# Float32r split of the row maxima moved from GpSimd to VectorE in an attention and expert kernel

## The reference

```python
xn = _layernorm(x)
q = xn @ Wq + bq;  latent = xn @ Wl + bl
k = latent @ Wk + bk;  v = latent @ Wv + bv          # 16 heads of 8
attn = softmax(q k^T * SCALE);  a = (attn v) @ Wo + bo
# experts: top 2 of 16, gate = min(gate, 7), up = clip(up, -7, 7)
out_e = ((up + 1) * gate * sigmoid(gate * 1.702)) @ Wd + bd
x = x + a + sum_e cw[e] * out_e
```

## Time and profile before

| | |
|---|---|
| three executions | 516.75, 517.58, 518.36 us |
| the profiled execution | 515.9 us, span of its instructions 514.0 us |
| TensorE busy | 453.2 us (88%), 2681 matmuls |
| VectorE busy | 374.6 us (73%) |
| ScalarE busy | 309.4 us (60%) |
| GpSimd busy | 192.9 us (38%) |
| mean granted TensorE clock | 0.913 |

### The profile page before, as it was taken

How to read it: one execution, slowest core, us unless ns; L and a number is a source line. 1 busy time by engine, 2 the same in 40 slices (tenths; PEclk the granted TensorE clock), 3 DMA queues, 4 the chain that set the end, 5 groups by cost and what they waited for, 6 DMA issues and landing times.

```text
span 514.0 us, 8995 instructions
## 1 busy us (share of the span) xinstructions
PE 453.2 (88%) x2681; PEld 209.3 (41%) x2681; DVE 374.6 (73%) x725; ACT 309.4 (60%) x356; POOL 192.9 (38%) x240
## 2 busy tenths in 40 slices
PE   0998984998989899989898989898989889799885
PEld 0554441333434344444444444444444434353243
DVE  8479992768888888888888878888888776764011
ACT  1541022477777686768686868686868644448840
POOL 6035876004141414141414141414141461824870
PEclk9976557789999999999999999999999988979966
DMA  8465512500544655304502443041004020101200
GB/s 239 126 120 179 101 44 87 162 3 1 129 123 121 189 102 111 104 1 78 109 22 83 86 100 104 3 82 22 21 3 91 16 59 7 39 22 43 57 23 25
DMA packets 39298, 39.01 MB, mean 76 GB/s; under 512 B 4998, under 2 KB 34792, under 8 KB 38376
## 3 DMA queue, kind: packets, MB, share of 16 engines
q1 hardware_dynamic: 35808, 33.74, 26.3%
q0 software_dynamic: 2432, 4.72, 3.9%
q10 hardware_dynamic: 1032, 0.23, 0.3%
HBM read 23.73 MB, written 13.89 MB: 73 GB/s over the span
## 4 chain that ended last, share of the span: by engine, by line
PE 59%; POOL 11%; DVE 11%; ACT 8%; issue 6%; another core or an unknown queue 2%; DMA 1%; ACTq 0%; SPq 0%; DVEq 0%; POOLq 0%
PE banks L987 17%; PE banks L970 16%; PE banks L1035 11%; DVE half_max L810 7%; ACT probs L674 5%; PE banks L1056 3%; PE banks L1054 3%; POOL th L545 2%; POOL up L546 2%; POOL up L528 2%; PE banks L1019 1%; PE banks L1017 1%; POOL th L544 1%; POOL up L541 1%
## 5 line engine op out<-in xcount | busy, mean ns | idle before, releaser
L810 DVE TENSOR_REDUCE half_max<-banks 128x1 f32<-128x512 f32 x512 | 322.0, 685 | 52.9 <-PE banks L970 39.9
L674 ACT ACTIVATE probs<-banks 128x1024 f32<-128x1024 f32 x256 | 254.9, 1026 | 162.5 <-PE banks L1035 113.1
L970 PE MATMUL banks<-k_rows,q_rows 62*128 62x512 f32 x512 | 182.9, 484 | 14.6 <-DVE half_max L810 10.4
L1035 PE MATMUL banks<-q_rows,k_rows 64*128 64x512 f32 x512 | 141.7, 460 | 7.0 <-ACT probs L674 5.5
L987 PE MATMUL banks<-probs,v_pad 128*32 128x512 f32 x1024 | 142.4, 630 | 0.0
L970 PEld LDWEIGHTS banks<-k_rows,q_rows 62*128 62x128 f32 x512 | 87.9, 199 | 103.5 <-DVE half_max L810 72.0
L1035 PEld LDWEIGHTS banks<-q_rows,k_rows 64*128 64x128 f32 x512 | 63.1, 192 | 77.6 <-ACT probs L674 66.9
L528 POOL TENSOR_TENSOR gate<-gate,w_blk 128x512 f32<-128x512 f32 x12 | 12.6, 1048 | 108.3 <-ACT gate L658 108.3
L528 POOL TENSOR_TENSOR up<-up,w_blk 128x512 f32<-128x512 f32 x12 | 12.6, 1049 | 97.8 <-ACT up L660 97.8
L510 POOL DMA_INDIRECT x_table<-xn,place_u x32 | 31.1, 972 | 20.9 <-DVE place_u L792 11.5
L987 PEld LDWEIGHTS banks<-probs,v_pad 128*32 128x32 f32 x1024 | 20.7, 110 | 44.3 <-issue 35.3
(11 more groups left out here) (117 smaller groups left out, 345.2 us busy)
## 6 DMA issues: line engine op xcount, KB each, us to landing
w_blk<-in_wexp SPq DMA_DIRECT2D x48, 193.0 KB, 3.1
q_rows<-q_parts SPq DMA_DIRECT2D x28, 128.0 KB
k_rows<-k_parts SPq DMA_DIRECT2D x56, 64.0 KB
x_table<-zeros SPq DMA_DIRECT2D x1, 3072.0 KB, 12.5
x_rows<-x_table SPq DMA_DIRECT2D x12, 256.0 KB, 3.7
moe_table<-x_rows SPq DMA_DIRECT2D x12, 256.0 KB, 6.8
q_parts<-q SPq DMA_DIRECT2D x8, 256.0 KB
k_parts<-k SPq DMA_DIRECT2D x8, 256.0 KB
```

The costliest lines, as they stand in the source:

```text
L674: nc.scalar.activation(probs[:, (2 * s + part) % 4, :, :], banks[:, bank:bank + 2, :], ACT.Exp, scale=SCALE).then_inc(slot_free, 1)
L810: nc.vector.tensor_reduce(half_max[:, unit, row, half:half + 1], banks[:, ring_bank(job), :], AX_X, ALU.max).then_inc(ring_free, 1)
L970: pe.matmul(bank, q_rows[slot][rows, pair, q0:q0 + P], k_rows[slot][rows, pair, 512 * keys:512 * keys + 512], start=True, stop=True).then_ ...
L1035: mm = pe.matmul(banks[:, bank + u, :], k_rows[(unit // 2) % 2][rows, pair, P * kb:P * kb + P], q_rows[(unit // 2) % 2][rows, pair, 512 * ...
```

## The change

The two GpSimd instructions of `split_max` and its two calls go. VectorE makes the first part itself, by a second reduction of the same 32 columns that writes float32r directly into `max2`, and then subtracts. Between the two it waits on its own semaphore `s_negmax`, which now counts two for each unit. The semaphore `s_vz` is no longer used, and `max_job` gets the turn `t` as a further argument. TensorE's, ScalarE's and SyncE's lists are the same.

```diff
             def split_max(parity, done):
-                pool.wait_ge(s_negmax, done)
-                whole = neg_max[:, parity, :].rearrange("p (u r) -> p u r", u=2)
-                nc.gpsimd.tensor_tensor(max2[:, parity, :, 0, :], whole, zeros[:, 0:16].rearrange("p (u r) -> p u r", u=2),
-                                        ALU.add).then_inc(s_vz, 1)
-                pool.wait_ge(s_vz, done)
-                nc.gpsimd.tensor_tensor(max2[:, parity, :, 1, :], whole, max2[:, parity, :, 0, :].bitcast(F32),
-                                        ALU.subtract).then_inc(s_max2, 1)
-                pool.wait_ge(s_max2, done)
...
             for n in range(2 * TILES):
-                    split_max(0, 1)
...
             def pair(t, p, last):
-                if has_max_turn(p, last):
-                    unit = (2 * p + LEAD - 2) // KB
-                    split_max(unit % 2, 4 * t + unit + 1)
...
-            def max_job(base, job, ahead, m):
+            def max_job(base, job, ahead, m, t):
...
                     nc.vector.tensor_reduce(neg_max[:, unit, :], half_max[:, unit, :, :], AX_X, ALU.max,
                                             negate=True).then_inc(s_negmax, 1)
+                    nc.vector.tensor_reduce(max2[:, unit, :, 0, :], half_max[:, unit, :, :].rearrange("p (u r) k -> p u r k", u=2),
+                                            AX_X, ALU.max, negate=True).then_inc(s_negmax, 1)
+                    dve.wait_ge(s_negmax, 8 * t + 2 * (ahead // KB) + 2)
+                    nc.vector.tensor_tensor(max2[:, unit, :, 1, :], neg_max[:, unit, :].rearrange("p (u r) -> p u r", u=2),
+                                            max2[:, unit, :, 0, :].bitcast(F32), ALU.subtract).then_inc(s_max2, 1)
```

More of the change, by code:

```diff
@@ L282, in moe_attention_kernel @@
         s_first_k = sem("s_first_k")
-        s_vz = sem("s_vz")
         s_vpad = sem("s_vpad")
@@ L484, in fill_v @@
                     v_all[:, bass.ds(g, 1), :, :].rearrange("p o k (j d) -> p (o k) j d", d=DH)).then_inc(s_vpad, 1)
-            def split_max(parity, done):
-                pool.wait_ge(s_negmax, done)
-                whole = neg_max[:, parity, :].rearrange("p (u r) -> p u r", u=2)
-                nc.gpsimd.tensor_tensor(max2[:, parity, :, 0, :], whole, zeros[:, 0:16].rearrange("p (u r) -> p u r", u=2),
-                                        ALU.add).then_inc(s_vz, 1)
-                pool.wait_ge(s_vz, done)
-                nc.gpsimd.tensor_tensor(max2[:, parity, :, 1, :], whole, max2[:, parity, :, 0, :].bitcast(F32),
-                                        ALU.subtract).then_inc(s_max2, 1)
-                pool.wait_ge(s_max2, done)
             pool.wait_ge(s_krow[0], 2)
@@ L852, in _ @@
                     maxima_turned(BEFORE_JOBS, TURN_OF_FIRST - BEFORE_JOBS, 0)
-                max_job(BEFORE_JOBS, job - BEFORE_JOBS, ahead, m)
+                max_job(BEFORE_JOBS, job - BEFORE_JOBS, ahead, m, 0)
             def pair(base, job, t, p, last):
@@ L857, in pair @@
                 for n, (ahead, m) in enumerate(maxima[:5]):
-                    max_job(base, job + n, ahead, m)
+                    max_job(base, job + n, ahead, m, t)
                 job += len(maxima[:5])
```

## The result

The changed kernel takes 521.51 us, the median of 20 executions (516.52 to 525.35). The kernel before took 517.62 us beside it (median of 20, 514.11 to 522.36). The ratio is 1.0066, with a 95% interval of 1.004 to 1.0093: slower by 0.7%, and outside the range of the forecast. The profiled execution has a span of 520.1 us and took 521.86 us; that of before had 514.0 and 515.9.

The account below looks back on a forecast made before the run. TensorE was taken as the bound (59% of the chain of waits), partly waiting for GpSimd's late split. Loop 9.0 - 1.6, plus 0.6 at the head, gave 8.0 us: 517.58 - 8.0 = 509.6 us, range 505.8 to 514.5.

Parts of the forecast that it names:

- The step that failed: Last turn: the last chain goes over TensorE, not the gathers, so gathers starting at once change 0, within 1.5 us.
- Rival 3: Head or last turn: the head's stop stays, or gathers running together hold up VectorE or ScalarE; 1 to 3 us lost; 12%.
- The loop: Three loop turns: nine TensorE waits for GpSimd's split shrink, gaining 9.0 us, less 1.6 us for delay on VectorE.
- The held subtraction: VectorE's two-input subtraction beside GpSimd's instructions in the loop: a possible wait for GpSimd, counted as nothing in the sum.
- Rival 1: Loop: the subtraction waits until GpSimd's running L544 ends, 0.37 or 0.52 us late, 3.8 us in all; 511.8 us; 34%.
- The register delay: VectorE in the loop: waiting on a register-held value delays the run of five 0.2 us, eight times, 1.6 us.
- the bare sum of 0.42: VectorE in the loop: reduction, wait and subtraction let the next max job start 0.42 us behind L814 at the shortest.
- The 9.0: Loop: the gain in us from nine TensorE waits at the transpose of the maxima, before VectorE's delays.
- Rival 2: Loop: the subtraction also waits for GpSimd's next instruction, L545; run of five 1.74 us late, 524.9 us; 6%.
- The head: First unit: without the split among GpSimd's scatters, these and VectorE's long stop come earlier; 0.6 us gained, between 0 and 0.9.
- The range's ends: Whole kernel: 505.8 us with full 9.0, 0.9 at the head, 1.5 in the last turn; 514.5 with rivals 1 and 3.

Follow-up runs that it names:

- Giving back the brake: The changed kernel, with GpSimd again waiting for VectorE's reduced maxima at the two old places in the last turn: 506.04 us, ratio 0.9844.
- the last turn alone: The kernel before, with only the last turn's two splits moved from GpSimd to VectorE: 524.78 us, ratio 1.0224.
- the one-input version: The changed kernel, with a third reduction of the 32 columns in place of the subtraction: 516.92 us, ratio 1.006.
- the spread version of the kernel before: The kernel before, split still on GpSimd, with gathers spread over the last turn's pairs and a pause in the head's scatters: 506.18 us, ratio 0.9843.
- the unaltered kernel: The changed kernel itself, run again in a set where the kernel before took 492.84 us: 487.01 us, ratio 0.9862.

## Why the prediction was wrong, step by step

**The step that failed** is the one on the last turn: "the last chain goes over TensorE to `y` at 510.61 us [...] not over the gathers, so I put this at 0, within 1.5 either way". It measured +12.7 us, the sum of +12.2, +10.4 and -9.9 in its three stretches. The argument looked only at whether somebody waits for the gathers' data. It missed that the gathers, while they are issued, stop the engines that set the time, and that TensorE's clock falls beside the stops. Moreover showed two waits of 11.12 and 13.42 us that would vanish with 16 gathers queued behind them, and the earlier trace rows had shown beside the scatters, which are such DMAs too, a stop of 9.66 us. With its price read from there, one such stop in the last turn would have forecast some 9 us more, 518 to 519. That is near to what came, but partly by luck: several stops and the slower clock lost more, and the end of the last turn gave 9.9 us back. Giving back the brake (0.9844) against the last turn alone (1.0224) shows this cause from both sides.

**Rival 3** had the mechanism in words, "gathers that now run together hold up VectorE or ScalarE", but was priced at 1 to 3 us and given 12%. Its argument against itself, "that the gathers stood beside the same work before", did not hold: they had stood beside it parted.

**The loop** went by the sum. It forecast 9.0 - 1.6 = 7.4 us; the milestones give 6.7. Where a wait had been, two transposes are 24.6 us apart instead of 25.4 (324.73 to 349.34 after, 330.35 to 355.74 before), close to the forecast 0.8. The first pass of the loop varies by some us between profiles of one and the same list (the second transpose to the 14th takes 301.4 to 309.3 us in the kernels with the change), so one pair of profiles proves little here. The later passes don't vary: from the 8th transpose to the 12th, a whole turn with three of the nine places, takes 101.7 to 101.8 us in all three kernels that keep the split on GpSimd in the loop and 99.4 to 99.6 in the 15 that have the change with its subtraction. That is 2.3 us a turn, 6.9 in three.

**The held subtraction.** The rule of the Trainium skill, SBUF — State Buffer, on engine ports was right here (0.40 to 0.58 us beside L532 against 0.17), and I had put the sum on the other side. Rival 1's sign came true: L805 ends with GpSimd's instruction. Two turns, GpSimd's row first:

```profile
122.45 0.62 POOL L532 TENSOR_SCALAR th<-th 128x512 f32<-128x512 f32 x1
147.11 0.62 POOL L532 TENSOR_SCALAR th<-th 128x512 f32<-128x512 f32 x1
...
146.90 0.19 DVE L800 TENSOR_REDUCE neg_max<-half_max 128x16 f32<-128x32 f32 x1
147.21 0.54 DVE L805 TENSOR_TENSOR max<-neg_max,max 128x16 fp32r<-128x16 f32 x1
147.67 3.07 DVE L796 TENSOR_REDUCE half_max<-banks 128x1 f32<-128x512 f32 x5
```

L532 ends at 123.07 and L805 at 122.70 + 0.40 = 123.10; in the second turn the ends are 147.73 and 147.75. The wait is inside the instruction's length and not in a bracket before it. The run of five starts 0.64 and 0.77 us behind L800, where I forecast 0.4 to 0.8. But the loss of 0.37 to 0.52 us at each place that rival 1 took from it is too high: the one-input version takes 98.95 us from the 8th transpose to the 12th, 0.57 less than the changed kernel's 99.52, or 0.2 at each of the three places.

**The register delay** of 0.2 us, guessed, is not there: with one input the run of five starts 0.42 us behind L800, the bare sum of 0.42. Its 1.6 us and the held subtraction's 3 x 0.57 = 1.7 us happen to be of the same size, so that the loop came out right is in part luck. The 9.0 itself holds: with one input a turn gains 101.81 - 98.95 = 2.86 us, 8.6 in three.

**Rival 2** did not occur: no subtraction beside L532 lasts into L533.

**The head** gave nothing instead of 0.6 us. The scatters did resume 1.1 us earlier (64.47 us after, 65.54 before) and the stop of 9.66 us shrank to 3.50, at 83.31 us. But the first transpose came 1.7 us later (67.06 after, 65.32 before), with max matmuls there of 0.79 us, and the second at the same time as before. One profile of each can't say more.

**The range's ends** are off by 0.3 to 0.4 us against their own terms: 517.58 - 9.0 - 0.9 - 1.5 is 506.2, not 505.8, and rival 1 with 3 us of rival 3 is 514.8, not 514.5. The measured 521.51 lies beyond either.

## What to carry to other kernels

Before a wait is removed, list what is queued behind it and ask what that will do to others while it runs, not only who waits for its data; a wait of an idle engine can be a brake that spaces its DMAs. If the trace shows somewhere an unexplained stop beside one kind of work, as here beside the scatters, take its full length as the price of the same work elsewhere, and read the granted clock behind it. When the change is right and its side effect is not, keep the wait and move the work: one wait put back, at two places, gave 1.6% faster than the kernel before, where the change without it had been 0.7% slower.

## What the runs showed of the hardware

Indirect DMAs that GpSimd issues one after the other, each 0.94 us with 0.30 between, stopped VectorE for up to 9.3 us and ScalarE for up to 9.6 us at the same time. Plain loads of the same size, from SyncE or GpSimd, stopped neither. With the pause of 12.39 us in the stream the stop was 2.25 us.

The place of the stops speaks for the same cause. In the eleven profiles that have stops, VectorE and ScalarE have 48 gaps over 1.5 us whose releaser is "remote". Every one began while a stream of scatters or gathers was running; 36 ended 0.1 to 3.3 us behind the stream's last one, as 429.46 against 426.48 us above, and 12 while it still ran. The stop of 6.86 us in the last turn of the kernel before belongs to them: eight gathers run from 478.7 to 488.4 us, and VectorE goes on at 490.13. But 3.5 us of it are no stop, since VectorE waits 3.5 us for TensorE at the same instruction in every kernel of the sets without stops. For the same reason a gap of 16.70 us in the spread version of the kernel before, put down to "remote" too, is not counted: 12.6 us of it are there in those kernels as well.

The stops are not in all runs. In three of the five sets of experiments, and in the runs of the result, the kernel before took 513 to 518 us and the profiles have them; in two sets it took 491.9 and 492.8, and no profile has a single one, at the head either, though the streams are as long. Each set of experiments ran on a chip of its own. Whether the chip or something else in the set decides was not tried.

Why an indirect DMA does this stays open. In the list of DMA queues for the stretch from 415 to 440 us, the profile after shows one packet of 16 KB on a queue named "instruction" beside the gathers:

```profile
q0 software_dynamic: 336, 0.66, 10.4%
q8 instruction: 1, 0.02, 0.3%
```

It lies at 421.0 us, inside the stop, which suggests that the stopped engines wait for a fetch of instructions that the gathers delay. The kept traces don't bear it out. Every profile has 12 such packets, six of them between 104 and 208 us, in the loop's first pass, where nothing stops and no indirect DMA runs; without gathers the packet comes at 418.6 us and nothing stops. In the kernel with only the last turn changed it comes at 438.2 us, behind a stop that lasted from 424.68 to 433.86, and at the head of the changed kernel at 90.7 us, behind one that ended at 83.31. No kernel changed the code's layout alone, so a fetch that these packets don't show is not ruled out.

A subtraction of 16 elements on VectorE took 0.17 us alone, 0.40 to 0.58 beside a one-input GpSimd instruction, and 1.67 in the unaltered kernel's second profile, where it began beside a gather and ended with L549 behind it.
